# A bound moved into a multiplication, an addition moved from GpSimd to VectorE, and the engines' step lists rewritten, in a two-layer local-attention kernel

## The reference

```python
for l in range(2):
    h = shift_token(x)                    # second half of the features from the token before
    q, k, v = split(h @ wqkv[l])          # 8 heads of 64
    q = q / clip(norm(q), 1e-12) * q_scale
    k = k / clip(norm(k), 1e-12) * k_scale
    q, k = rotary_xpos(q, k)
    o = local_attention(q, k, v)          # windows of 128, this one and the one before
    x = x + o @ wo[l]
    h = layernorm(shift_token(x)) * ln_g + ln_b
    a, g = split(h @ w1[l] + b1[l])
    x = x + (a * gelu(g)) @ w2[l] + b2[l]
out = x0 + gated_attention(xn) + x
```

## Time and profile before

| | |
|---|---|
| median of three runs | 1930.73 us (1926.85 to 1933.40) |
| profiled execution | 1927.33 us, span 1925.2 us, mean granted clock 0.984 |
| TensorE busy | 1823.5 us, 95% |
| ScalarE busy | 1374.2 us, 71% |
| VectorE busy | 1231.2 us, 64% |
| GpSimd busy | 881.4 us, 46% |

### The profile page before, as it was taken

How to read it: one execution, slowest core, us unless ns; L and a number is a source line. 1 busy time by engine, 2 the same in 40 slices (tenths; PEclk the granted TensorE clock), 3 DMA queues, 4 the chain that set the end, 5 groups by cost and what they waited for, 6 DMA issues and landing times.

```text
span 1925.2 us, 47714 instructions
## 1 busy us (share of the span) xinstructions
PE 1823.5 (95%) x17808; PEld 1565.2 (81%) x17808; DVE 1231.2 (64%) x4126; ACT 1374.2 (71%) x3998; POOL 881.4 (46%) x1302
## 2 busy tenths in 40 slices
PE   6999999999999879999999999999999999999998
PEld 4788788788778658888898897888888888889787
DVE  5543544445443357777777777787777777777765
ACT  5886978788688556857758668677576685775864
POOL 3533543344243455536436355364473553654631
PEclk9999999999999979999999999999999999999999
DMA  4321321322223620111101101314112112010110
GB/s 148 101 77 44 113 87 54 91 96 88 74 91 99 210 69 23 48 42 32 51 26 45 57 15 53 107 33 163 45 40 64 34 48 65 23 59 26 43 48 29
DMA packets 125018, 128.11 MB, mean 67 GB/s; under 512 B 26632, under 2 KB 100082, under 8 KB 124788
## 3 DMA queue, kind: packets, MB, share of 16 engines
q1 hardware_dynamic: 121620, 118.77, 19.9%
q10 hardware_dynamic: 3168, 6.29, 1.0%
HBM read 72.44 MB, written 36.85 MB: 57 GB/s over the span
## 4 chain that ended last, share of the span: by engine, by line
PE 75%; ACT 10%; DVE 6%; POOL 3%; DMA 2%; SPq 2%; issue 1%; DVEq 0%; POOLq 0%; ACTq 0%
PE f_bank L1454 18%; PE a_bank L630 16%; PE f_bank L1593 10%; PE f_scores L1608 5%; PE f_o_bank L1568 5%; PE a_o_bank L727 4%; PE f_scores L1535 4%; ACT f_prob L1677 3%; PE f_bank L1546 3%; PE a_bank L712 2%; PE a_scores L704 2%; PE f_bank L1507 2%; POOL a_prob L610 2%; PE f_bank L1550 1%; DVE f_u L1817 1%
## 5 line engine op out<-in xcount | busy, mean ns | idle before, releaser
L1418 POOL TENSOR_SCALAR f_prob<-f_prob,f_row_inv 128x192 f32<-128x192 f32 x512 | 224.4, 457 | 391.9 <-DVE f_row_inv L1759 391.9
L610 POOL TENSOR_SCALAR a_prob<-a_prob,a_row_inv,a_gate 128x128 f32<-128x128 f32 x512 | 226.3, 459 | 377.5 <-DVE a_row_inv L948 377.5
L1454 PE MATMUL f_bank<-weights,f_actT 128*128 128x512 f32 x1152 | 300.8, 407 | 1.6 <-DVE f_actT L1710 1.6
L1593 PE MATMUL f_bank<-f_hT,f_w 128*128 128x256 f32 x2112 | 269.1, 283 | 1.1 <-DVE f_gu L1813 1.1
L1593 PEld LDWEIGHTS f_bank<-f_hT,f_w 128*128 128x128 f32 x2112 | 258.5, 188 | 4.1 <-DVE f_gu L1813 2.7
L1454 PEld LDWEIGHTS f_bank<-weights,f_actT 128*128 128x128 f32 x1152 | 210.8, 191 | 46.9 <-DVE f_actT L1710 1.8
L1677 ACT ACTIVATE f_prob<-f_scores,f_neg_max 128x192 f32<-128x192 f32 x512 | 208.0, 427 | 17.7 <-DVE f_neg_max L1751 16.4
L1406 POOL TENSOR_TENSOR f_qk_tok<-f_qk_tok,tables 128x512 f32<-128x512 f32 x128 | 164.5, 1305 | 116.3 <-DVE f_sin_part L1727 116.3
L1697 ACT ACTIVATE f_u<-f_gu 128x256 fp32r<-128x256 f32 x192 | 80.2, 418 | 174.1 <-DVE f_gu L1813 174.1
L1400 POOL TENSOR_TENSOR f_norm<-f_norm,f_minus_half 128x16 f32<-128x16 f32 x64 | 187.7, 2933 | 32.2 <-DVE f_norm L1719 31.4
L838 ACT ACTIVATE a_prob<-a_scores,a_neg_max 128x128 f32<-128x128 f32 x512 | 179.4, 391 | 24.1 <-DVE a_neg_max L939 24.0
(11 more groups left out here) (143 smaller groups left out, 3958.6 us busy)
## 6 DMA issues: line engine op xcount, KB each, us to landing
split_weights<-a_hi_lo SPq DMA_DIRECT2D x16, 512.0 KB, 3.0
x_next<-states SPq DMA_DIRECT2D x32, 256.0 KB, 3.2
tables<-scaled_tables SPq DMA_DIRECT2D x16, 512.0 KB, 5.9
f_x<-states SPq DMA_DIRECT2D x16, 512.0 KB, 5.1
split_weights<-a_hi_lo SPq DMA_DIRECT2D x12, 682.0 KB, 4.7
weights<-split_weights ACTq DMA_DIRECT2D x6, 1024.0 KB, 9.5
f_w<-split_weights SPq DMA_DIRECT2D x4, 1280.0 KB, 10.7
f_v_crossed<-f_v SPq DMA_DIRECT2D x40, 128.0 KB, 2.4
```

What stands on the lines that cost most here:

```text
L610: last = nc.gpsimd.tensor_scalar(part, part, row_inv[:, a % 2, head, t:t + 1], gate[:, half, t, h:h + 1], ALU.mult, ALU.mult)
L1418: last = nc.gpsimd.tensor_scalar(part, part, row_inv[:, a % 2, head, t:t + 1], 1.0, ALU.mult, ALU.mult)
L1454: last = nc.tensor.matmul(out, lhs(c, a), rhs(c, b), start=(i == 0), stop=(i == len(order) - 1))
L1593: mm = nc.tensor.matmul(out[:, which * PART:(which + 1) * PART], w1[:, wp, c, col:col + P], hT[:, hp, c, columns_of(a // FH)], start=(i == ...
```

## The change

Four things:

1. `sum_squares` has no clamp any more. The bound is applied after the power: `rope_sum` takes the smaller of the norm's power and 1e12 and multiplies by it, in one `scalar_tensor_tensor` in place of the `tensor_tensor`. GpSimd's power now waits for the sum of squares itself.
2. `add_attended` moves from GpSimd to VectorE.
3. The tables of all engines are rewritten. On TensorE `transpose_x` goes ahead of `scores` 1, `values` 2 behind `scores` 6, `down` 4, 5 and 6 and `up` 7 and 9 change places. On ScalarE `take_o` 1 goes ahead of `transpose_qk` 0. On VectorE `rope` 3 goes behind `up` 4. On GpSimd the power of `project_qk` 2 goes ahead of `weigh` 5, that of `project_qk` 3 to the end.
4. On SyncE `load_x` goes from the head of a chunk to behind `cross_values`, and `shift_keys` ahead of `shift_front`.

```diff
-                ("softmax", 5), ("transpose_qk", 0), ("take_o", 1), ("transpose", 4), ("softmax", 6), ("project_qk", 3), ("transpose", 5),
+                ("softmax", 5), ("take_o", 1), ("transpose_qk", 0), ("transpose", 4), ("softmax", 6), ("project_qk", 3), ("transpose", 5),
...
-                ("up", 2), ("ln_apply", 1), ("up", 3), ("transpose_h", 1), ("rope", 3), ("up", 4), ("up", 5), ("up", 6), ("up", 7),
-                ("up", 8), ("up", 9), ("rope_sum", 3), ("up", 10), ("up", 11), ("out", 0), ("out", 1)]
+                ("up", 2), ("ln_apply", 1), ("up", 3), ("transpose_h", 1), ("up", 4), ("rope", 3), ("up", 5), ("up", 6), ("up", 7),
+                ("up", 8), ("up", 9), ("rope_sum", 3), ("up", 10), ("up", 11), ("add_attended", 0), ("out", 0), ("out", 1)]
...
             def norms(it, a):
 
-                pool.wait_ge(clamped.sem, clamped.past(it, ("project_qk", a)))
+                pool.wait_ge(emptied.sem, emptied.past(it, ("project_qk", a), KEY))
                 n = norm[:, a % TILES].rearrange("p i h -> p (i h)")
                 nc.gpsimd.tensor_tensor(n, n, minus_half[:], ALU.pow).then_inc(norm_ready.sem, 1)
...
-                elif kind == "add_attended":
-                    pool.wait_ge(attended_loaded.sem, attended_loaded.past(it, (kind, a)))
-                    pool.wait_ge(ln_scaled.sem, ln_scaled.past(it, ("ln_apply", 2 * a + 1)))
...
-                        nc.gpsimd.tensor_tensor(x1[:], x1[:], x_tok[:], ALU.add).then_inc(attended_added.sem, 1)
...
-                dve.wait_ge(emptied.sem, emptied.past(it, ("project_qk", a), KEY))
-                nc.vector.tensor_scalar(norm[:, a % TILES], norm[:, a % TILES], 1e-24, None, ALU.max).then_inc(clamped.sem, 1)
-
             def rope(it, a):
...
                 dve.wait_ge(rope_added.sem, rope_added.past(it, ("rope_sum", a)))
-                nc.vector.tensor_tensor(by_head(place), by_head(place), norm[:, a % TILES].unsqueeze(3).broadcast_to([P, 2, F_HEADS, DH]),
-                                        ALU.mult).then_inc(roped.sem, 1)
+                nc.vector.scalar_tensor_tensor(out=by_head(place), in0=norm[:, a % TILES].unsqueeze(3).broadcast_to([P, 2, F_HEADS, DH]), scalar=1e12,
+                                               in1=by_head(place), op0=ALU.min, op1=ALU.mult).then_inc(roped.sem, 1)
...
+                elif kind == "add_attended":
+
+                    if a == 0:
+                        dve.wait_ge(edge_kept.sem, edge_kept.past(it, ("shift_keys", 0)))
+                        dve.sem_inc(dve_carried, 1)
+                    if layer:
+                        dve.wait_ge(attended_loaded.sem, attended_loaded.past(it, (kind, a)))
+                        dve.wait_ge(ln_scaled.sem, ln_scaled.past(it, ("ln_apply", PARTS * a + 1)))
+                        nc.vector.tensor_tensor(x1[:], x1[:], x_tok[:], ALU.add).then_inc(attended_added.sem, 1)
+                    else:
+                        dve.sem_inc(attended_added.sem, 1)
```

More of the change, by code:

```diff
@@ L992 @@
 F_FIRST_HALF = ("shift_keys", "load_wqkv", "load_others")
[L993 to L1004, removed]
-         ("down", 5), ("down", 6), ("transpose_qk", 2), ("up", 10), ("up", 11), ("down", 7), ("down", 8),
-         ("add_attended", 0), ("transpose_qk", 3), ("down", 9), ("out", 0), ("out", 1), ("down", 10), ("down", 11)]
@@ L1007 @@
-SYNC_ORDER = [("load_x", 0), ("load_x1", 0), ("load_tables", 0), ("load_others", 0), ("shift_front", 0), ("shift_keys", 0),
-              ("shift_back", 0), ("cross_values", 0), ("add_attended", 0), ("out", 0), ("out", 1)]
+ORDER = [("softmax", 0), ("scores", 0), ("scores", 1), ("weigh", 0), ("weigh", 1), ("softmax", 1), ("transpose_x", 0), ("scores", 2),
+         ("transpose", 0), ("softmax", 2), ("transpose", 1), ("scores", 3), ("weigh", 2), ("project_qk", 0), ("softmax", 3), ("values", 0),
+         ("take_o", 0), ("load_x1", 0), ("weigh", 3), ("rope", 0), ("values", 1), ("scores", 4), ("transpose", 2), ("project_qk", 1),
+         ("softmax", 4), ("scores", 5), ("transpose", 3), ("weigh", 4), ("rope_sum", 0), ("project_qk", 2), ("values", 2), ("scores", 6),
+         ("softmax", 5), ("weigh", 5), ("rope", 1), ("take_o", 1), ("values", 3), ("transpose_qk", 0), ("transpose", 4), ("scores", 7),
+         ("softmax", 6), ("weigh", 6), ("project_qk", 3), ("project_o", 0), ("transpose", 5), ("softmax", 7), ("values", 4), ("values", 5),
+         ("rope_sum", 1), ("load_tables", 0), ("load_others", 0), ("weigh", 7), ("take_o", 2), ("ln_stats", 0), ("transpose", 6),
+         ("project_v", 0), ("transpose_qk", 1), ("transpose", 7), ("ln_apply", 0), ("take_o", 3), ("rope", 2), ("values", 6), ("values", 7),
+         ("project_v", 2), ("transpose_h", 0), ("project_o", 1), ("rope_sum", 2), ("shift_keys", 0), ("shift_front", 0), ("up", 0),
+         ("up", 1), ("ln_stats", 1), ("up", 2), ("project_v", 1), ("down", 0), ("down", 1), ("project_v", 3), ("ln_apply", 1), ("up", 3),
+         ("down", 2), ("transpose_h", 1), ("rope", 3), ("up", 4), ("down", 3), ("up", 5), ("up", 6), ("up", 7), ("down", 4),
+         ("shift_back", 0), ("up", 8), ("down", 5), ("up", 9), ("rope_sum", 3), ("load_x", 0), ("cross_values", 0), ("transpose_qk", 2),
+         ("down", 6), ("up", 10), ("up", 11), ("down", 7), ("down", 8), ("down", 9), ("transpose_qk", 3), ("add_attended", 0), ("out", 0),
+         ("out", 1), ("load_wqkv", 0), ("down", 10), ("down", 11)]
@@ L1165, in layers_phase @@
         raw_taken = count("raw_taken", {"project_qk": 2})
-        clamped = count("clamped", {"project_qk": 1})
         norm_ready = count("norm_ready", {"project_qk": 1})
```

22 lines of the change are left out of this document (9 added, 13 removed).

## The result

| | before | after |
|---|---|---|
| median | 1929.76 us (four runs, 1926.85 to 1933.40) | 1947.42 us (four runs, 1944.49 to 1948.78) |
| profiled execution, its span | 1927.33, 1925.2 us | 1944.49, 1942.7 us |
| mean granted clock | 0.984 | 0.978 |
| TensorE / VectorE / ScalarE / GpSimd busy | 1823.5 / 1231.2 / 1374.2 / 881.4 us | 1832.8 / 1209.7 / 1378.9 / 852.1 us |

The ratio is 1.0089, with an interval of 1.0067 to 1.0111: the changed kernel is slower, by 17.7 us in the medians and 17.5 us in the spans of the two profiled executions. The forecast was 1936, and the range ended at 1944. VectorE and GpSimd lost 21 and 29 us of work, and it bought nothing.

The account below looks back on a forecast made before the run. TensorE's fixed matmuls, some 74 of each chunk's 76.7 us, were taken as the bound, with only 2.5 us at its start and waits near its end winnable. Terms summed to +7.0 us, giving 1936 us, range 1924 to 1944.

Parts of the forecast that it names:

- ahead of the first chunk: In the preparation, which passes through one clamp: its removal was to gain 0 to 0.4 us, taken as -0.2 us.
- `transpose_x`: later weighing: Chunk starts: `scores` 1 delayed, GpSimd's weighing later, `transpose` 1 ends 0.5 us later in four full-clock layer 0 starts, +2.0 us.
- `transpose_x`: clock: Eight low-clock chunk starts: `transpose_x` ahead of the wait runs at full clock, -0.35 us each after later weighing, -2.8 us.
- `values` 2: `project_qk` 2 waits for VectorE's sum of squares: 3.5 us in second-half chunks, 1.6 us in first-half chunks, +5.1 us.
- addition, layer 1: Chunk ends: 0.7 us gained off GpSimd, handed back at the next start with 0.2 more; +0.15 us in seven chunks, +1.0 us.
- end of a chunk, layer 0: `up` 9 behind `down` 5 makes the last `up` 0.7 us later; `down` 11 pays 0.15 us, eight times, +1.2 us.
- very end: At the kernel's end the addition stands ahead of the last two `out`: 0 to 1.2 us, taken as +0.7 us.
- Run ahead of the wait it is at full clock.: Chunk starts: `transpose_x`, 1.97 us instead of 1.09 behind the wait, was to save that 0.88 us, less 0.5 for later weighing.
- the clock falls at every start: Rival: low clock also in the seven full-clock starts, over the transposes behind the weighing, 5.6 us above forecast, 1942; chance 0.12.
- the clamp: On VectorE, 26.1 us of instructions removed; TensorE waits for nothing behind it, so worth 0 in the chunks.
- The new multiplication: On VectorE with the bound inside: 1.30 us against 1226 ns, 4.7 us of VectorE in all, nothing on the path.
- the releases win: Rival: bank free when TensorE comes, starts cost nothing, half of layer 1's 0.7 us comes through; -5.5 us, 1925; chance 0.28.

Follow-up runs that it names:

- e8: The kernel before with sixteen more transposes, dead work, in the pause ahead of `scores` 2: 1922.31 us, ratio 0.9973.
- e12: The changed kernel with eight dead transposes ahead of `scores` 2 and eight ahead of `transpose` 0 of each chunk: 1929.30 us, 1.0006 to the kernel before.
- e4: The kernel before with only `transpose_x` moved ahead of `scores` 1 on TensorE: 1943.28 us, ratio 1.0081.
- e9: The kernel before with only `values` 2 moved behind `scores` 6 on TensorE: 1929.74 us, ratio 1.0013.
- e7: The kernel before with `transpose_x` moved between `scores` 1 and `scores` 2 on TensorE: 1926.93 us, ratio 1.0004.
- e1: The changed kernel with `transpose_x` put back behind `scores` 2 on TensorE: 1933.89 us, 1.0029 to the kernel before.
- e6: The kernel before with only the addition of the kept rows moved to VectorE, between `up` 11 and `out` 0: 1924.68 us, ratio 0.9985.
- e5: The kernel before with only the clamp removed and the bound put inside the multiplication: 1928.71 us, ratio 1.0003.
- e14: The changed kernel with TensorE's and ScalarE's lists of the kernel before: 1932.28 us, 1.0017 to the kernel before.
- e13: The changed kernel with all of TensorE's list of the kernel before: 1937.00 us, 1.0048 to the kernel before.

## Why the prediction was wrong

The sign was right, the size was not: +7.0 us was said, +17.5 measured, and two terms, the clock and the addition, have the wrong sign. The clock is separated by the two filled kernels: e8 has a span of 1918.5 us against 1925.2 before, 6.7 us; e12 has 1928.6 against 1942.7 after, 14.1 us. So by the spans 7.4 of the 17.5 us are the clock and 10.1 us come at full clock. This split is not sharp. By the ratios (1.0089, 1.0006 and 0.9973 to the kernel before) it is about 10.8 and 6.4 us. In the fourteen middle chunks alone it is 5.3 and 5.7 us; the two ends, where executions differ most, hold the rest. Both parts are there in every reading, and over the whole kernel the clock is 7 to 11 us of it.

| step | forecast | measured |
|---|---|---|
| ahead of the first chunk | -0.2 | +0.7 (within scatter) |
| `transpose_x`: later weighing | +2.0 (0.5 in 4 chunks) | +7.4 (0.49 in 15, from the one start of e4 at full clock) |
| `transpose_x`: clock | -2.8 | +7.4 by the spans, +10.8 by the ratios |
| `values` 2 | +5.1 | +2.1 (e9) |
| addition, layer 1 | +1.0 | -3.2 to -3.6 |
| end of a chunk, layer 0 | +1.2 | +0.5 (8 x 0.07) |
| very end | +0.7 | +1.6 |
| sum | +7.0 | +16.1 to +16.5 with the clock by the spans, of 17.5 |

**The step that failed: "Run ahead of the wait it is at full clock."** That holds for `transpose_x` itself, and the step stopped there. It took the low clock for something that happens to the instruction behind the wait. It isn't: the wait stayed, so the low clock came as often (9 starts for 8), only later, and fell on `scores` 3 and `project_qk` 0, which nothing hides. Before, an affected start cost mostly 0.7 to 0.9 us, since part of the slow work lay in front of the waits of 0.41 and 0.16 us for VectorE; after, it costs up to 1.3 us in layer 0 and 2.0 to 2.3 in layer 1, where the low stretch is twice as long (6.8 us and not 3.4). The term of -2.8 should have been positive. The rival "the clock falls at every start" named this mechanism and this place, with 0.12; its price of 0.8 us a start was too low for layer 1, and its "every start" is nearly what e4 shows (13 of 15) and the changed kernel does not (9).

The Trainium skill (TensorE: Matmul & The Clock Gate, Part 1) ties the clock to recent activity. The runs agree, in both directions: with rest in the start, in one piece (before) or in several (e4, e7), the granted clock falls to 0.50 in many of the starts, and with dead transposes in its place (e8, e12) it is 1.00 through all fourteen chunks. Three pieces of rest under 1 us each can be enough, which e7 shows; they are not enough every time.

**The later weighing** had the right size, 0.50 us, and the wrong count. In eight starts it was set off against a clock gain that did not exist, and in layer 1 it was thought to lie beside the delay by the addition. It does: `scores` 1 behind `transpose_x` hardly waits for `out` 1 any more (1.5 us in two places, e1 8.0 us in seven). But then it is the weighing that costs, and the term has to be paid in all fifteen.

**`values` 2.** The delay of 0.5 us exists, fifteen times. The step said that "nothing later in a second-half chunk takes that up", and this was wrong by half: `values` 2 is 0.16 us cheaper next to `values` 3, and the stretch behind `transpose_qk` 0 gives 0.11 back (e9). In first halves 0.06 reaches the end of A, where 0.2 was taken.

**The addition.** That GpSimd's addition costs 0.7 us a chunk was right: C is 18.17 in e6 and 18.24 after. "So the gain of 0.7 is handed back at the start of the next chunk, and 0.2 more" was wrong. Alone, it hands back only part (e6, -3.4 us). In the changed kernel the hand-back and the later weighing lie beside each other: A at full clock is 0.13 and 0.12 us longer in layer 1 than in layer 0, in the twelfth chunk 0.46. That is -7 x 0.63 + 7 x 0.12 = -3.6 us, or -3.2 with the 0.46 once.

**Right:** the clamp is worth nothing (e5, 1.0003). The new multiplication is off the path; at 1226 ns it costs just what the old one did, not 1.30 us, and the 17 that ran beside GpSimd's power took no longer than the other 47. `project_qk` 2 waits in fifteen chunks, `transpose` 0 and 1 wait for GpSimd, and the wait of `scores` 2 is 0.97 us in layer 0 (1.51 in layer 1).

**The rival "the releases win"** fell: the bank was not free, the starts were not free, and of the gains only the addition's came through, and more of it than the half that the rival took.

**Still open.** Of the 17.5 us 1.0 to 1.4 are in no term, and the terms are no sharper than that. VectorE's lateness of 0.4 us in layer 1 (e14 against e6) was not traced to one entry of a list. What brings the low clock in one start and not in another with the same pauses is not known, nor why the low stretch is twice as long in layer 1 of the changed kernel and of e13 than in e4.
